# A fused two-layer block on one core: 64-row score products for the row maxima, and a later wait for the low part of the query

## What is computed

```python
q_big = jnp.einsum('bshk,hkq->bshq', q_hk, w_kc_q)
kv_rope = kv_c * cos[None] + _rotate_half(kv_c) * sin[None]
q_r = jnp.einsum('bshq,hqr->bhsr', q_big, W_qr)
k_r = jnp.einsum('bld,hdr->bhlr', kv_rope, W_kr)
scores = jnp.einsum('bhsr,bhlr->bhsl', q_r, k_r)
attn = jax.nn.softmax(scores, axis=-1)
ctx_c = jnp.einsum('bhsl,bld->bhsd', attn, kv_rope)
```

## Time and profile before

| | |
|---|---|
| median of 3 runs | 474.0 us (473.12 to 474.25) |
| span of the profiled execution | 472.4 us, 7935 instructions |
| PE busy | 401.0 us (85%), 2691 matmuls |
| PEld busy | 332.9 us (70%) |
| DVE busy | 325.9 us (69%) |
| ACT busy | 235.2 us (50%) |
| POOL busy | 135.7 us (29%) |
| L1347, 128 matmuls | 32.7 us, 351 ns mean |
| L1307, 192 matmuls | 32.0 us, 288 ns mean |
| L1837, 64 reductions | 41.3 us, 686 ns mean |
| granted TensorE clock, mean | 0.948 |

### The profile page before, as it was taken

How to read it: one execution, slowest core, us unless ns; L and a number is a source line. 1 busy time by engine, 2 the same in 40 slices (tenths; PEclk the granted TensorE clock), 3 DMA queues, 4 the chain that set the end, 5 groups by cost and what they waited for, 6 DMA issues and landing times. The chain is left out here.

```text
span 472.4 us, 7935 instructions
## 1 busy us (share of the span) xinstructions
PE 401.0 (85%) x2691; PEld 332.9 (70%) x2691; DVE 325.9 (69%) x772; ACT 235.2 (50%) x515; POOL 135.7 (29%) x140
## 2 busy tenths in 40 slices
PE   1669896758899988998988898778998799999996
PEld 0335594437689777888778796668897677778885
DVE  0889849454899458998559995668772357555885
ACT  1013667326369546497465695553365344444331
POOL 4815100004301137102046011244268910001730
PEclk9999978878579999999999999998999899999999
DMA  6995700093011001010011010030354422211320
GB/s 157 291 328 186 101 2 0 9 311 102 1 24 24 3 0 46 1 26 22 1 25 24 2 45 1 2 90 24 89 186 150 145 80 89 90 46 46 111 92 22
DMA packets 30743, 35.37 MB, mean 75 GB/s; under 512 B 5712, under 2 KB 25792, under 8 KB 30448
## 3 DMA queue, kind: packets, MB, share of 16 engines
q1 hardware_dynamic: 26304, 28.11, 19.7%
q0 software_dynamic: 4400, 6.75, 6.4%
HBM read 25.61 MB, written 7.60 MB: 70 GB/s over the span
## 5 line engine op out<-in xcount | busy, mean ns | idle before, releaser
L1753 DVE RECIPROCAL egh<-egh 128x256 bf16<-128x256 bf16 x44 | 76.5, 1740 | 2.0 <-ACT egh L920 2.0
L1388 PE MATMUL bank<-kv,probs 128*128 128x128 f32 x512 | 67.5, 275 | 3.4 <-ACT negmT L981 2.9
L1388 PEld LDWEIGHTS bank<-kv,probs 128*128 128x128 f32 x512 | 62.5, 192 | 4.1 <-issue 4.1
L1008 ACT ACTIVATE probs<-bank 128x512 f32<-128x512 f32 x64 | 36.9, 587 | 16.9 <-PE bank L1368 16.9
L1837 DVE TENSOR_REDUCE negm<-bank 128x2 f32<-128x512 f32 x64 | 41.3, 686 | 4.0 <-PE bank L1347 3.6
L1347 PE MATMUL bank<-Kh,Qs 128*128 128x256 f32 x128 | 32.7, 351 | 9.7 <-DVE negm L1837 4.8
L1367 PE MATMUL bank<-Qs,Kh 128*128 128x256 f32 x128 | 39.4, 329 | 0.0
L733 POOL TENSOR_SCALAR veps<-mv 128x2 f32<-128x2 f32 x12 | 2.7, 226 | 126.1 <-DVE mv L1584 126.1
L916 ACT ACTIVATE gu_all<-bank 128x512 bf16<-128x512 f32 x44 | 26.0, 590 | 24.0 <-PE bank L1171 23.8
L1550 PEld LDWEIGHTS bank<-W,hTs 128*128 128x128 f32 x210 | 28.1, 189 | 13.3 <-DVE hTs L1991 7.6
L1550 PE MATMUL bank<-W,hTs 128*128 128x256 f32 (+1 forms) x210 | 32.9, 293 | 3.8 <-DVE hTs L1991 2.6
(11 more groups left out here) (205 smaller groups left out, 890.7 us busy)
## 6 DMA issues: line engine op xcount, KB each, us to landing
Qm<-Qs SPq DMA_DIRECT2D x32, 128.0 KB
xs<-f3A SPq DMA_DIRECT2D x1, 2432.0 KB, 9.9
Qm<-xs SPq DMA_DIRECT2D x19, 128.0 KB, 2.1
ys<-y SPq DMA_DIRECT2D x19, 128.0 KB, 2.0
w_q<-in_wq SPq DMA_DIRECT2D x2, 1024.0 KB, 17.6
w_o<-in_woT SPq DMA_DIRECT2D x1, 2048.0 KB, 11.4
w_in<-in_L_ffn_Wg SPq DMA_DIRECT2D x8, 256.0 KB, 5.0
w_in<-in_L_ffn_Wu SPq DMA_DIRECT2D x8, 256.0 KB, 3.0
```

Of the source, the lines that this page charges most:

```text
L1008: done(act.activation(flat(pT[:, n % 3]), bank1(b, FILL_ST + h)[:], ACT.Exp), "p_ready")
L1388: ins = pe.matmul(bank_v(b, h // 2)[:, at:at + P], pT[:, n % 3, lt, t * P:(t + 1) * P], kv_all[:, frm:frm + P], start=(lt == 0), stop=(lt ...
L1753: done(dve.reciprocal(eg[:, j], eg[:, j]), "e1")
```

## The change

The score products for the maxima read the 64 partitions in which the high part of the head's query lies, and the same 64 of `Kh`: the low part of the query no longer enters the maxima. They wait for `q_hi` in place of `q_split`. The complete scores, which still read both parts, wait for `q_split` once in four heads. GpSimd waits at the end of a batch's `rows_split` until its own subtractions are complete.

```diff
--- before.py
+++ after.py
@@ -810,6 +810,7 @@
                         lo = slice(DC * (1 - par), DC * (1 - par) + DC)
                         less(flat(Qs[lo, par, 2 * n:2 * n + 2]), full[(SPLITS * b + n) % 2][hi],
                              flat(Qs[hi, par, 2 * n:2 * n + 2]), "q_split")
+                own(pool, "q_split")
 
             def ctx_split(b, ks):
 
@@ -1342,9 +1343,10 @@
                 for h in range(NH):
                     par, pr = h % 2, h // 2
                     bk = wait_fill1(pe, b, FILL_S + h)
-                    pe.wait_ge(S_["q_split"], 8 * b + 2 * (pr // 2 + 1))
+                    pe.wait_ge(S_["q_hi"], 8 * b + 2 * (pr // 2 + 1))
+                    half = slice(DC * par, DC * par + DC)
                     for t in range(T):
-                        ins = pe.matmul(bk[:, t * S:(t + 1) * S], Qs[:, par, pr, t * P:(t + 1) * P], Kh[:, kb],
+                        ins = pe.matmul(bk[:, t * S:(t + 1) * S], Qs[half, par, pr, t * P:(t + 1) * P], Kh[half, kb],
                                         start=True, stop=True)
                     done(ins, "s_ready")
                     if h == NP + 1:
@@ -1361,6 +1363,7 @@
                     bk = wait_fill1(pe, b, FILL_ST + h)
                     if h % 4 == 0:
                         qm_loaded(pe, 4 * b + h // 4)
+                        pe.wait_ge(S_["q_split"], 8 * b + 2 * (h // 4 + 1))
                     for t in range(T):
                         o = bk[:, t * S:(t + 1) * S]
                         kt = slice(b * S + t * P, b * S + (t + 1) * P)
```

## The result

The changed kernel takes **506.3 us** (median of four runs, 506.02 to 507.26) against 474.03 (473.12 to 474.25) before: a ratio of 1.068, 95% interval 1.0665 to 1.0704. The profiled execution has a span of 504.7 us against 472.4. The forecast was 496.3 with a range of 481 to 511. The time lies in the range, and the sign and size are as forecast, but not the case that was called the likeliest: the clock fell in two stages and not in one, which is the rival at 508.2. Ratios and their intervals are of fast executions alone; two executions of the case were slow ones, 528.3 us of the kernel with everything on 64 rows and 497.5 us of the one with borders put in, and no reading rests on them.

A forecast was written before the change was run, and what follows sets the result against it. In the stages for the maxima TensorE and VectorE were both taken as just full. Borders and a cold batch 3 gave 0.8 + 6.6 + 14.9 = +22.3 us, 494.7 profiled, plus 1.6: 496.3 us, range 481 to 511.

The forecast's parts named there:

- the case that was called the likeliest: Batch 3's stage alone stays at half clock, batches 1 and 2 at full clock: 496.3 us, chance 0.35.
- the rival at 508.2: Batch 1 or 2 also falls to half clock and stays down: +11.9 us for one; cold in one more stage, chance 0.23.
- The wait that goes: Score products for the maxima no longer wait for GpSimd's split; worth 0, batch 3's wait of 1.84 us stays.
- the one that comes: In the complete scores TensorE waits for `q_split` once in four heads, 16 times; worth 0.
- The price of a border: Each switch between 64-row and 128-row matmuls: 0.18 us at full clock (0.15 to 0.20), 0.265 at half.
- Batch 2: Its stage at full clock, a head's step 0.95 us against 0.65: +3.3 us.
- Batch 0: No output products, only six borders at half clock, about half hidden under a VectorE reciprocal: +0.8 us, between 0 and 1.6.
- Batch 3: Clock stays at 1.2 GHz through the stage, step 1.60 us: +13.2, and +1.7 in the complete scores; together +14.9 us.
- the list of signs: What would show it: among others steps near 0.95 us at full clock, and clock 0.50 from batch 3's head 1.
- Batch 1: Its stage at full clock, two borders per head, step 0.95 us against 0.65: +3.3 us.
- The reason given for a clock that stays down: In batch 3's stage each head has two gaps at borders, and with gaps a fallen clock does not come back.

The follow-up runs named there:

- the kernel with everything on 64 rows: Changed kernel with the output projection also in 64-row products, twice as many, lower half of its contraction taken twice: 516.91 us, ratio 1.089.
- the one with borders put in: Kernel before, score products still on 128 rows, with a useless 64-row, 8-column product ahead of each head of batches 1 to 3: 492.06 us, ratio 1.0409.
- the 65-row run: Kernel before with the even heads' products for the maxima on 65 rows and the odd heads' on 128: 474.32 us, ratio 1.0007.
- the kernel with the old wait: Kernel before with its products for the maxima on 64 rows, the wait for the low part of the query left in place: 506.91 us, ratio 1.068.
- with the waits filled: Changed kernel with useless 128-row matmuls in TensorE's waits at the head of the stages of batches 1 to 3: 485.71 us, ratio 1.0223.
- paired output products: Changed kernel with the output products of two heads issued together behind the odd head, so half the borders: 486.30 us, ratio 1.0254.

## Why the prediction was right, and where it was not

**The wait that goes, and the one that comes: right.** Both at nothing. L1349's waits are the three kinds of the earlier trace rows, batch 3's on VectorE's copy is 1.6 us in place of 1.8, and keeping the old wait changes no stretch.

**The price of a border: right in kind, 10% low.** A head has five products of 0.118 us, 0.59; the step measures 0.98, so a border costs (0.98 - 0.59) / 2 = 0.195 us, where 0.18 was taken and 0.20 the high end. At half clock it is (1.66 - 1.07) / 2 = 0.295 against 0.265. The steps were forecast at 0.95 and 1.60. The Trainium skill's TensorEngine Tiling, Key Properties, has the mode switch drain TensorE without a time. The trace agrees, and the 65-row run shows where it stops: in the even heads, which alone were changed there, one row more and the 0.39 us per head are gone.

**Batch 2: right.** +4.4 measured for +3.3 forecast. The stage itself, from its first head to the complete scores, takes 17.85 us instead of 14.26, +3.6. The other 0.8 lie behind it and need not be the change's: the 65-row kernel, whose stage takes 14.28, has 69.34 us from batch 2 to batch 3 where the kernel before has 68.14. **Batch 0: too high,** +0.2 for +0.8; no run looks at its six borders by themselves.

**Batch 3: right in kind, and close because errors cancel.** +14.7 for +14.9. Its stage takes 26.2 us (335.69 to 361.86) against 13.8, +12.3 for a forecast of 13.2, and +2.4 lie behind it for 1.7. The sum had all fifteen steps from head 1 on at half clock, and the list of signs had 0.50 from there; but the first two ran at full clock (0.99 and 0.98), the third was under way when the clock fell (1.51), and the other twelve took 1.66 for 1.60. The clock returned at 367 to 368, not 3.5 but 6 us after the complete scores began.

**Batch 1: the term that failed.** It stood in the sum as a warm stage, +3.3; it took +13.8. The prediction named the two waits and the gaps that come on top, and gave the case "cold in one more stage" 0.23 against 0.35. So 496.3 was 10.0 us low, nearly all of it here, and the time is inside the range because the range took this rival in. The price of the rival, 11.9 us, was 1.6 too high: the stretch takes 79.63 us cold and 69.38 with the waits filled, 10.3 more, all of it in the stage (28.20 and 17.85 us), and the 1.7 forecast for behind the stage did not come. What could have moved the weights was in the rows, though only hindsight says how far: in the kernel before, the stage of batch 0 fell to 0.50 with waits between products at full rows, and batch 3 fell after 1.84 us; a stage with shorter waits and two open loads per head lies nearer to them than a stage with short waits alone.

**The reason given for a clock that stays down fell.** It said: the gaps of the borders keep it there. With no gaps, on 64 rows, it stayed down for 22 us in batch 1 and 20 in batch 3. Whether such gaps could keep it down between 128-row products stays open: in the profile of the run made for that the clock never fell there. The forecast of batch 3 came out by a cause that was in part another. What the runs support: a low clock came back in 3 to 4 us when half the score products had 128 rows, in about 10 (batch 1) and in 4 to 5 (batches 2 and 3) with half the borders, and not within 20 us in the changed kernel or in the one that ran on 64 rows alone. A full clock stayed full on the same 64-row work wherever the head of the stage had been carried over: filled by work of either kind, or at 128 rows. The Trainium skill's TensorE: Matmul & The Clock Gate, Part 1, lets sustained work lift the clock. In the stretch at 188 to 210 us of the run with everything on 64 rows TensorE had work all the time and the clock stayed at 0.50, so the measurement speaks against that rule for half rows, or at least for these 64-row float32 products.

**Left open.** Why batch 1 fell and batch 2, with waits equal to 0.01 us, did not. It is no accident of one execution: the profiles of the kernel with the old wait, of the one with 64 rows in the even heads and of the one with everything on 64 rows show the same, and only with paired output products did batch 2 fall too. Open also is which share of the fall is the empty time at the borders and which the missing rows: the borders alone (the run with 128 rows) tip it sometimes at most.

## What to carry to other kernels

Reading fewer rows saves no time on TensorE; at 64 or fewer beside products of 128 each change of shape costs 0.2 us, so keep such products at 65 rows or more or group them. Read the granted clock of every stage and not the busy share, and when a change adds small gaps to a stage that begins with waits, price the stage at half clock too. Where TensorE waits for another engine in a stage whose clock is low, useless products into a free piece of a bank can pay: here 0.9% of the kernel, most of it in one stage.

## What the hardware showed that was not expected

- A border depends on one row: 65 rows beside 128 cost nothing (474.3 us), 64 rows in the same half of the heads cost 8.5 us more (482.9).
- Both levels of the clock can hold on the same work: in one execution of the kernel with everything on 64 rows, products of 64 rows ran at 0.50 from 188 to 210 us and at 1.00 from 266 to 276 us.
- Three heads of 128 rows at the start of a stage, 3.8 us (183.96 to 187.75), are as good as filling its waits: 486.3 against 485.7 us. They kept the clock over a wait of 1.85 us, and all four executions lie within 485.5 to 487.1, while the kernel before lost it over 1.84 us in its profiled execution and the 65-row kernel kept it over 1.83. The same wait can go either way.
